# Keys and queries of two batches made ahead of the loop, and unread products on TensorE

## The chip, the core and the metric

The kernel runs on one core of a Trainium2 chip. The metric is the device time of one execution in microseconds (us). The kernel before takes 330.56 us, the median of three runs (330.47 to 331.02). The profile is one further execution of 328.42 us, whose span on the core is 326.3 us.

The engines are TensorE (PE; its weight loads are PEld), VectorE (DVE), ScalarE (ACT), GpSimd (POOL) and SyncE (SP), which only issues transfers. Each takes its instructions in the order in which the program has them and stops at a wait until a semaphore reaches a value.

## The reference, cut to what matters

```python
# x [8,112,256], ctx [8,375,256], 16 heads of 16, mask [8,1,112,375]
q = heads(layernorm(x) @ Wq + bq); k = heads(ctx @ Wk + bk); v = heads(ctx @ Wv + bv)
scores = where(mask, -1e15, q k^T / 4)
x = x + tanh(g_xattn) * (heads_back(softmax(scores) v) @ Wo + bo)
h = layernorm(x)
# router: mean over the rows -> tanh(@W1 + b1) -> @W2 + b2 -> softmax -> the best 3 of 8 zones, per batch
x = x + tanh(g_ffn) * (h + sum over those 3 zones of w * (gelu(h @ Wa[zone]) @ Wb[zone]))
```

## The kernel before

A batch is one of the eight samples. The program has two parts. A loop over `b` from -2 to 7 does attention, and at the same time turns the weights of all eight zones (`Wa`, `Wb`) into a high and a low half in fp16 that stay in SBUF. A second stage does the 24 zone products, three a batch.

The loop is pipelined by hand over batches. In iteration `b` the kernel makes the keys and queries of batch `m = b + 2`, the raw scores and row maxima (`s1`, L1016; `row_max`, L769) and the values of batch `n = b + 1`, and the transposed scores, exponentials and sums with the values of batch `b` (`st_tile`, L1028 and L1032; `exp_tile`, L545; `pv`, L1048). What belongs to the output of batch `b - 1` follows (names with `o`). So iteration -2 makes only keys and queries of batch 0, iteration -1 the scores of batch 0 with the keys and queries of batch 1 between them, and iteration 0 is the first with exponentials. Every iteration has four slots. `slot_uses` lists which small products stand in a slot, and the class `Spare` deals three PSUM banks out to them in that order; a product waits until the one that had its bank before is read.

How keys and queries are made: TensorE transposes the context (CX0, CX1, L1057) and the normalized x (XT, L1083), ScalarE and VectorE copy them out (`cx_copy`, `xt_copy`), TensorE multiplies with Wk and Wq (K0, K1, L1066; Q, L1092), ScalarE writes the fp16 high part and VectorE the low part (`k_hi`, `k_lo`, `q_hi`, `q_lo`). SyncE writes them to DRAM (`write_k`, L316; `write_q`, L310) and reads them back in another layout in two groups of six transfers (`read_k`, L339; `read_q`, L327). The first score product of a batch waits for the first group.

SyncE's queue carries nearly all transfers of the loop: these, the context (L299), x (L292) and mask (L304) of coming batches, the expert weights, two parts of 128 x 512 at a time, into a ring of six (`load_parts`, L359 and L362), and the move of the row maxima into `rq` (`move_max`, L348). The weights start in iteration -1: parts 0 to 3 are asked for in its slots 0 and 1 and worked on in slots 2 and 3. For each pair GpSimd scales (`scale_part`, L459), ScalarE rounds to the high half (`w_hi`, L655), and GpSimd subtracts to the low half (`lo_part`, L464). GpSimd scales the pair of the next slot before it makes the low halves of the present one. The normalization of x of the batch after next stands at the end of an iteration: statistics on VectorE (`ln1_stats`, L788 to L791), two operations on GpSimd (`norm1`, L469 and L470), then `normed` (L586) on ScalarE. All of this is in program order on each engine, so ScalarE starts the exponentials of iteration 0 only behind `w_hi` of parts 0 to 3 and `normed`.

The constants: ScalarE's queue loads Wq, Wk, bk, bq, bv, the gates and Wo ahead of all its work. `tanh_gates` (L611, L615) takes the gates and scales Wo at the end of iteration -2. GpSimd loads bo and the router's small weights (L502 to L506) ahead of the loop. The product of bv with Wo (BO, L1102) stands in slot 3 of iteration -1. VectorE fills five tiles with constants at the start (L897 to L902), counted by `zeroed`.

Of the kernel before, what the change touches and what calls it, by code (L numbers as in the profile page):

```python
# [11 lines left out]
ACT = mybir.ActivationFunctionType  # L12
# [48 lines left out]

def slot_uses(b, slot):

    n, m, o = b + 1, b + 2, b - 1
# [6 lines left out]
    more = {(B - 2, 3): ("H", 0), (B - 1, 0): ("L", 0), (B - 1, 2): ("W", 0), (-1, 3): ("BO", 0)}.get((b, slot))  # L71
# [16 lines left out]
class Spare:  # L88


    def __init__(self):
        names, banks = [], []
# [48 lines left out]
def flamingo_layer(nc, x, ctx, mask, g_xattn, g_ffn, Wq, bq, Wk, bk, Wv, bv, Wo, bo,  # L141
                   W1, b1, W2, b2, Wa, Wb, out):
    with ExitStack() as stack:
# [143 lines left out]
        def _(sp):  # L287
# [111 lines left out]
            load_ctx(0)  # L399
            sp.dma_start(wqkvo[:, 2, :, :], view_w(Wv)).then_inc(s["wv_loaded"], 16)  # L400
            for b in range(-2, B):
                n, m, o = b + 1, b + 2, b - 1
                read_k(n, 1)
                read_q(n, 1)
# [3 lines left out]
                load_ctx(m + 1)  # L408
                load_x(m + 1)
                load_mask(m)  # L410
                load_parts(b, 1)
# [39 lines left out]
        def _(pool):  # L451
# [46 lines left out]
            pool.wait_ge(s["zeroed"], 5)  # L498
# [3 lines left out]
            g.dma_start(bo_r[:, :], bass.AP(bo.tensor, 0, [[0, 128], [1, D]])).then_inc(s["const_loaded"], 16)  # L502
            g.dma_start(w1_s[:, :, :], W1.rearrange("(t p) n -> p t n", p=128)).then_inc(s["const_loaded"], 16)
            g.dma_start(w2_s[:, :], W2).then_inc(s["const_loaded"], 16)
            g.dma_start(b1_c[:, :], b1.rearrange("(p o) -> p o", o=1), allow_slow_non_contiguous=True).then_inc(s["const_loaded"], 16)
            g.dma_start(b2_r[:, :], bass.AP(b2.tensor, 0, [[0, B], [1, NZ]])).then_inc(s["const_loaded"], 16)  # L506
            for b in range(-2, B):
                for slot in range(4):
# [9 lines left out]
                    for k in ks:  # L518
                        lo_part(k)
            norm2(B - 2)  # L520
# [4 lines left out]
        def _(act):  # L525
            a = nc.scalar
            a.dma_start(wq_in, view_w(Wq)).then_inc(s["wq_loaded"], 16)
            a.dma_start(wqkvo[:, 1, :, :], view_w(Wk)).then_inc(s["wk_loaded"], 16)
            a.dma_start(bk_c[:, :], bk.rearrange("(t p) -> p t", p=128), allow_slow_non_contiguous=True).then_inc(s["bk_loaded"], 16)
            for t in range(DT):  # L530
                a.dma_start(bq_c[:, t:t + 1], bass.AP(bq.tensor, t * 128, [[1, HD], [HD, PAIRS], [1, 1]]), allow_slow_non_contiguous=True).then_inc(s["bq_loaded"], 16)
            a.dma_start(bv_c[:, :], bv.rearrange("(t p) -> p t", p=128), allow_slow_non_contiguous=True).then_inc(s["bv_loaded"], 16)
            a.dma_start(gates[:, 0:1], bass.AP(g_xattn.tensor, 0, [[0, 128], [1, 1]])).then_inc(s["g_loaded"], 16)
            a.dma_start(gates[:, 1:2], bass.AP(g_ffn.tensor, 0, [[0, 128], [1, 1]])).then_inc(s["g_loaded"], 16)
            a.dma_start(wqkvo[:, 3, :, :], view_w(Wo)).then_inc(s["wo_loaded"], 16)
# [38 lines left out]
            def mask_bias(b):  # L574
                if there(b):
# [3 lines left out]
                    if b == 0:  # L579
                        act.wait_ge(s["zeroed"], 5)  # L580
# [88 lines left out]
            normed(0)  # L669
            act.wait_ge(s["wq_loaded"], 16)  # L670
# [614 lines left out]
```

## Time and profile before

| what | us |
|---|---|
| median of the runs | 330.56 |
| profiled execution | 328.42 |
| its span | 326.3 |
| TensorE busy | 289.3 (89%) |
| VectorE busy | 203.2 (62%) |
| ScalarE busy | 195.5 (60%) |
| GpSimd busy | 134.3 (41%) |
| loop starts its iteration 0 (TensorE) | 42.45 |
| iteration 1 | 62.96 |
| zone products start | 198.62 |

The median lies 2.14 us above the profiled execution. Times below count from the start of the span. A row of a timeline merges equal instructions: where it starts, how long it lasts, engine and line, what it writes and reads, how many, and in brackets how long the engine stood idle before it and what ended that. PEq, SPq and ACTq are the sequencers, which issue transfers. A product of fp32 matrices counts as two instructions.

### The profile page before, as it was taken

The numbers are of one execution on the slowest core, as the hardware profiler recorded it, in microseconds if no ns is written. First come the engines' busy times: TensorE is split into PE (matmuls) and PEld (weight loads), VectorE is DVE, ScalarE is ACT, GpSimd is POOL, SyncE is SP. The second block draws the span as 40 slices with busy tenths as digits, with TensorE's granted clock in tenths as the row PEclk, the third lists the DMA queues.
The fourth block names the chain that finished last, engine by engine and source line by source line (L and its number), as shares of the span: only waits on it lengthen the run. The fifth ranks groups of instructions, "written<-read, shape, count | busy, mean of one in ns | idle before, by whom it ended". The sixth has DMA issues, their size and how long they took to land.

```text
span 326.3 us, 9360 instructions
## 1 busy us (share of the span) xinstructions
PE 289.3 (89%) x3348; PEld 242.0 (74%) x3348; DVE 203.2 (62%) x617; ACT 195.5 (60%) x406; POOL 134.3 (41%) x185
## 2 busy tenths in 40 slices
PE   1619679899989999999989867999999999999996
PEld 1406457676766766767666646999999999999996
DVE  7417838576787777877687545656564745636542
ACT  2413466877878778777787876635454753543531
POOL 3401576867778689687788871000000000000000
PEclk9978979999999999999999999999999999999999
DMA  7458776787677977868664512101110110101000
GB/s 163 123 152 234 177 226 161 214 250 182 196 206 176 274 211 191 255 182 242 180 191 145 147 44 58 33 27 33 41 33 2 44 31 17 44 2 44 2 16 14
DMA packets 39324, 40.51 MB, mean 124 GB/s; under 512 B 10249, under 2 KB 35137, under 8 KB 39281
## 3 DMA queue, kind: packets, MB, share of 16 engines
q1 hardware_dynamic: 37168, 38.94, 42.7%
q10 hardware_dynamic: 1936, 0.79, 1.0%
q8 instruction: 28, 0.46, 0.6%
q0 software_dynamic: 176, 0.20, 0.3%
q14 instruction: 16, 0.12, 0.1%
HBM read 33.09 MB, written 6.74 MB: 122 GB/s over the span
## 4 chain that ended last, share of the span: by engine, by line
PE 64%; DMA 9%; ACT 7%; DVE 5%; issue 5%; SPq 5%; POOL 2%; ACTq 0%; DVEq 0%
PE bank L1240 18%; PE bank L1221 16%; PE bank L1066 6%; PE bank L1075 4%; PE bank L1016 4%; DMA qbd<-q_scr 4%; PE bank L1028 4%; PE bank L1032 3%; PE bank L1048 3%; ACT pT L545 2%; DMA stage<-in_L_ffn_Wa 2%; PE bank L1057 2%; SPq L339 2%; PE bank L1132 2%; ACT wa L655 2%
## 5 line engine op out<-in xcount | busy, mean ns | idle before, releaser
L769 DVE CUSTOM_DVE_ANT_0 bank<-bank,maskb 112x375 f32<-112x375 f32 x128 | 67.9, 571 | 39.8 <-PE bank L1016 39.7
L1240 PE MATMUL bank<-wb,stage 128*112 x576 | 66.8, 273 | 0.0
L1240 PEld LDWEIGHTS bank<-wb,stage 128*112 128x112 f16 x576 | 62.2, 130 | 0.2
L1221 PE MATMUL bank<-ctxT,wqkvo 128*128 128x112 f16 x960 | 59.4, 213 | 2.0 <-DVE qbd L895 1.3
L1221 PEld LDWEIGHTS bank<-ctxT,wqkvo 128*128 128x128 f16 x960 | 57.5, 98 | 2.9 <-issue 2.2
L732 ACT ACTIVATE kst<-bank 128x448 f32<-128x448 f32 x48 | 25.6, 534 | 55.4 <-PE bank L1221 55.3
L545 ACT ACTIVATE pT<-bank 125x448 f32<-125x448 f32 x96 | 48.9, 539 | 9.0 <-PE bank L1032 8.3
L894 DVE COPY wqkvo<-wa 128x3072 f16 x24 | 23.2, 969 | 48.5 <-PE bank L1221 47.5
L459 POOL TENSOR_SCALAR stage<-stage 128x512 f32<-128x512 f32 x64 | 38.5, 618 | 26.5 <-DMA stage<-in_L_ffn_Wa 21.7
L1016 PE MATMUL bank<-kst,qbd 128*112 128x375 f16 x128 | 33.8, 338 | 15.2 <-DMA qbd<-q_scr 11.8
L464 POOL TENSOR_TENSOR wb<-stage,wb 128x512 f16<-128x512 f32 x32 | 37.5, 1191 | 14.0 <-ACT wb L655 14.0
L1028 PE MATMUL bank<-rq,maskb 115*128 115x448 bf16 (+1 forms) x96 | 35.5, 370 | 7.5 <-ACT pT L545 7.1
L1221 PE MATMUL bank<-ctxT,qbd 128*128 128x112 f16 x192 | 40.9, 213 | 0.0
L464 POOL TENSOR_TENSOR wa<-stage,wa 128x512 f16<-128x512 f32 x32 | 36.4, 1159 | 10.0 <-ACT wa L655 10.0
L1032 PE MATMUL bank<-qbd,kst 128*128 128x224 f16 (+1 forms) x192 | 34.4, 260 | 0.0
L958 DVE SCALAR_TENSOR_TENSOR stage<-kst,wbc,stage 128x448 f16<-128x448 f32 x48 | 30.9, 680 | 3.9 <-ACT stage L734 3.8
L734 ACT ACTIVATE stage<-kst,wbc 128x448 f16<-128x448 f32 x48 | 32.1, 669 | 1.6
L1032 PEld LDWEIGHTS bank<-qbd,kst 128*128 128x128 f16 (+1 forms) x192 | 21.6, 113 | 11.7 <-issue 1.3
L1016 PEld LDWEIGHTS bank<-kst,qbd 128*112 128x112 f16 x128 | 15.0, 132 | 19.9 <-DMA qbd<-q_scr 12.8
L1048 PE MATMUL bank<-pT,vp 125*17 125x112 f32 (+1 forms) x768 | 24.7, 261 | 0.0
L469 POOL TENSOR_TENSOR rstd<-ve,half 112x1 f32<-112x1 f32 x16 | 8.8, 551 | 37.0 <-DVE ve L791 37.0
L1028 PEld LDWEIGHTS bank<-rq,maskb 115*128 115x128 bf16 (+1 forms) x96 | 10.7, 111 | 14.9 <-ACT pT L545 12.7
(123 smaller groups left out, 423.6 us busy)
## 6 DMA issues: line engine op xcount, KB each, us to landing
stage<-in_L_ffn_Wa SPq DMA_DIRECT2D x16, 512.0 KB, 4.3
stage<-in_L_ffn_Wb SPq DMA_DIRECT2D x16, 512.0 KB, 4.4
kst<-k_scr SPq DMA_DIRECT2D x64, 93.8 KB, 3.7
k_scr<-wb SPq DMA_DIRECT2D x16, 187.5 KB
ctx_s<-in_ctx SPq DMA_DIRECT2D x8, 336.0 KB
qbd<-q_scr SPq DMA_DIRECT2D x32, 56.0 KB, 3.1
xa<-in_x SPq DMA_DIRECT2D x8, 112.0 KB, 4.4
q_scr<-wb SPq DMA_DIRECT2D x16, 56.0 KB, 3.2
```

Of the source, the lines that this page charges most:

```text
L459: g.tensor_scalar(st, st, WSCALE, 1.0, ALU.mult, ALU.mult).then_inc(s["scaled"], 1)
L464: g.tensor_tensor(part_dst(k, 1), stage[:, k % RING, :], part_dst(k, 0), ALU.subtract).then_inc(s["lo_done"], 1)
L545: a.activation(pT[0:CK, t % PRING, :], bank[0:CK, ST_BANKS[t % len(ST_BANKS)], 0:QUAD], ACT.Exp).then_inc(s["act_exp"], 1)
L734: a.activation(hT[:, u % 2, cols], h_w[:, cols], ACT.Copy, scale=wbc[:, u:u + 1]).then_inc(s["hthi_done"], 1)
L769: v.tensor_tensor_reduce(out=bank[0:SQ, e, 0:SK], in0=bank[0:SQ, e, 0:SK], in1=maskb[0:SQ, b % 2, 0:SK], scale=-1.0, scalar=FLOOR, op0=ALU ...
L958: v.scalar_tensor_tensor(out=hT[:, u % 2, (2 + hf) * QUAD:(3 + hf) * QUAD], in0=h_w[:, cols], scalar=wbc[:, u:u + 1], in1=hT[:, u % 2, col ...
L1016: T.matmul(bank[0:SQ, e, 0:SK], qbd[:, b % 2, e, p, :], kst[:, b % 2, p * SK:(p + 1) * SK], start=True, stop=True).then_inc(s["pe_s1"], 1)
L1028: T.matmul(o[0:w, :].rearrange("k (j q) -> k j q", j=4), maskb[0:KQ, b % 2, c * CK:c * CK + w], rq[0:KQ, g // 2, :, g % 2, :], start=True, ...
L1032: ins = T.matmul(o[0:w, i * 2 * SQ:(i + 1) * 2 * SQ].rearrange("k (e q) -> k e q", e=2), kst[:, b % 2, p * SK + c * CK:p * SK + c * CK + w ...
L1048: ins = T.matmul(bank[32 * j:32 * j + VC, O_BANK, g * SQ:(g + 1) * SQ], vp[0:k, b % 2, c, h, :], pT[0:k, tile(b, g, c) % PRING, j * SQ:(j ...
L1221: ins = T.matmul(o, first(ws, t, f), x2b[:, b % 2, (xs * DT + t) * SQ:(xs * DT + t + 1) * SQ], start=(t == 0 and xs == 0 and ws == 0), sto ...
L1240: ins = T.matmul(o, hT[:, u % 2, hs * FT * SQ + f * SQ:hs * FT * SQ + (f + 1) * SQ], wb[:, bass.ds(e * (4 * CHUNK) + ws * (2 * CHUNK) + f ...
```

## The change

Keys and queries of batches 0 and 1 are made in a row ahead of the loop, in the order of the list `AHEAD`, on all engines. The loop starts at -1. In iteration -1 nothing is made of keys and queries (`made(-1)` is no batch); from iteration 0 on they are made of `b + 2` as before. On SyncE the write and the reads of batch 1 stand ahead of the loop, so ahead of the first weights. Wk is loaded ahead of Wq; bk and bq move from ScalarE's queue to SyncE's, ahead of the mask of batch 0; Wv moves behind the reads of batch 0; bv, the gates and Wo move to SyncE's queue in iteration -1. GpSimd's five constant loads move to the end of iteration -1, `tanh_gates` there too, and the product BO with what VectorE does with it to iteration 0. VectorE's fills of vp and pT move behind batch 0's keys and queries. A function `busy(n)` on TensorE multiplies the identity with itself into a score bank; nothing reads the result. It runs nine times ahead of the first transposes and twelve times behind batch 1's queries.

```diff
+def made(b):
+    return b + 2 if b >= 0 else B
...
+AHEAD = (("CX0", 0), ("CX1", 0), ("XT", 0), ("K0", 0), ("K1", 0), ("Q", 0),
+         ("CX0", 1), ("CX1", 1), ("K0", 1), ("K1", 1), ("XT", 1), ("Q", 1))
...
             load_x(0)
             load_ctx(0)
+            sp.dma_start(bk_c[:, :], bk.rearrange("(t p) -> p t", p=128), allow_slow_non_contiguous=True).then_inc(s["bk_loaded"], 16)
...
+            load_mask(0)
+            load_ctx(1)
+            load_x(1)
+            write_k(0, 0)
+            write_k(0, 1)
+            write_q(0)
+            for h in range(2):
+                read_k(0, h)
+                read_q(0, h)
             sp.dma_start(wqkvo[:, 2, :, :], view_w(Wv)).then_inc(s["wv_loaded"], 16)
-            for b in range(-2, B):
-                n, m, o = b + 1, b + 2, b - 1
-                read_k(n, 1)
-                read_q(n, 1)
+            load_mask(1)
+            write_k(1, 0)
+            write_k(1, 1)
+            write_q(1)
+            for h in range(2):
+                read_k(1, h)
+                read_q(1, h)
+            for b in range(-1, B):
+                n, m, o = b + 1, made(b), b - 1
+                if n > 1:
+                    read_k(n, 1)
+                    read_q(n, 1)
                 move_max(b, 1)
                 load_parts(b, 0)
                 load_xr(o)
-                load_ctx(m + 1)
-                load_x(m + 1)
+                load_ctx(b + 3)
+                load_x(b + 3)
                 load_mask(m)
+                if b == -1:
+                    sp.dma_start(wqkvo[:, 3, :, :], view_w(Wo)).then_inc(s["wo_loaded"], 16)
...
                 load_parts(b, 1)
...
+                    if (b, slot) == (-1, 3):
+                        g.dma_start(bo_r[:, :], bass.AP(bo.tensor, 0, [[0, 128], [1, D]])).then_inc(s["const_loaded"], 16)
...
             normed(0)
+            cx_copy(0)
+            xt_copy(0)
             act.wait_ge(s["wq_loaded"], 16)
...
+            k_hi(0, 0)
+            k_hi(0, 1)
+            q_hi(0)
+            cx_copy(1)
+            mask_bias(0)
+            normed(1)
+            k_hi(1, 0)
+            k_hi(1, 1)
+            xt_copy(1)
+            q_hi(1)
+            mask_bias(1)
...
-                normed(m + 1)
-                if b == -2:
+                normed(b + 3)
+                if b == -1:
                     tanh_gates()
...
             v.memset(qbd[:].rearrange("p a e j f -> p (a e j f)"), 0.0).then_inc(s["zeroed"], 1)
+            ln1_stats(0)
+            v.memset(bank[:, O_BANK, :], 0.0).then_inc(s["zeroed"], 1)
+            v.memset(maskb[96:KQ, :, :], 1.0).then_inc(s["zeroed"], 1)
+            cx_copy(0)
...
+            def busy(n):
+                for i in range(n):
+                    T.matmul(bank[:, ST_BANKS[i % 2], 0:128], ident[:, :], ident[:, :], start=True, stop=True)
...
             pe.wait_ge(s["ident_ready"], 1)
-            pe.wait_ge(s["zeroed"], 3)
-            for b in range(-2, B):
+            busy(9)
+            for name in AHEAD:
+                put(name)
+            busy(12)
+            for b in range(-1, B):
```

What stands in a row on SyncE before, from the last read of batch 0 to the write of batch 1 (`stage` takes expert weights, `k_scr` and `q_scr` are keys and queries in DRAM, `kst` and `qbd` the tiles that they are read back to):

```order
L327 DMA qbd<-q_scr 64x1x448 x2
L359 DMA stage<-in_L_ffn_Wa 128x1024
L299 DMA ctx_s<-in_ctx 112x3x256
L299 DMA ctx_s<-in_ctx 13x3x256
L292 DMA xa<-in_x 112x256
L304 DMA mask_s<-in_mask_Bx1xSxS_bk 112x375
L359 DMA stage<-in_L_ffn_Wa 128x1024
L316 DMA k_scr<-wb 8x32x375 x2
L310 DMA q_scr<-wb 128x2x112 x2
L348 DMA rq<-ms 3x4x224
```

And now, from the same read to the first weights:

```order
L335 DMA qbd<-q_scr 64x1x448 x2
L420 DMA wqkvo<-in_L_xattn_Wv 128x2x256
L312 DMA mask_s<-in_mask_Bx1xSxS_bk 112x375
L324 DMA k_scr<-wb 8x32x375 x2
L318 DMA q_scr<-wb 128x2x112 x2
L347 DMA kst<-k_scr 32x1500 x4
L335 DMA qbd<-q_scr 64x1x448 x2
L347 DMA kst<-k_scr 32x1500 x4
L335 DMA qbd<-q_scr 64x1x448 x2
L367 DMA stage<-in_L_ffn_Wa 128x1024
```

The first weights stand directly behind batch 0's reads before, and behind batch 1's write and all twelve of its reads now. Behind them SyncE has now, to the second weights:

```order
L367 DMA stage<-in_L_ffn_Wa 128x1024
L307 DMA ctx_s<-in_ctx 112x3x256
L307 DMA ctx_s<-in_ctx 13x3x256
L300 DMA xa<-in_x 112x256
L440 DMA wqkvo<-in_L_xattn_Wo 128x2x256
L441 DMA bv_c<-in_L_xattn_bv 128x2x1
L442 DMA gates<-in_g_xattn 128x1
L443 DMA gates<-in_g_ffn 128x1
L367 DMA stage<-in_L_ffn_Wa 128x1024
L356 DMA rq<-ms 3x4x224
```

Four transfers that ScalarE's queue issued have come between, and the mask has gone. On ScalarE this stands before, from the values of batch 0 to the first exponentials (`pT`):

```order
L605 ACTIVATE vp<-bank,vsc 125x32x16
L655 ACTIVATE wa<-stage 128x512 x2
L581 ACTIVATE maskb<-mask_s 112x375
L605 ACTIVATE vp<-bank,vsc 126x16x16
L655 ACTIVATE wa<-stage 128x512 x2
L586 ACTIVATE xa<-xa,nmr,rstd 112x256
L545 ACTIVATE pT<-bank 125x448 x2
```

And now:

```order
L633 ACTIVATE vp<-bank,vsc 125x32x16
L683 ACTIVATE wa<-stage 128x512 x2
L633 ACTIVATE vp<-bank,vsc 126x16x16
L683 ACTIVATE wa<-stage 128x512 x2
L614 ACTIVATE xa<-xa,nmr,rstd 112x256
L639 ACTIVATE tgate<-gates 128x2
L643 ACTIVATE wqkvo<-wqkvo,tgate 128x512
L573 ACTIVATE pT<-bank 125x448 x2
```

The high halves of parts 0 to 3 stand ahead of the first exponentials in both; the gates and the scaling of Wo have joined them, and the mask has left.

## Rows read from the trace of the kernel before

**Rows 1.** Busy time by stretch: length, each engine (instructions), granted clock, DMA share, GB/s.
```profile
0.00:42.45 42.45, 20.88 (x86) 14.23 (x86) 23.45 (x71) 14.20 (x31) 14.62 (x32) 0.92 0.64 168
...
62.96:198.62 135.66, 126.18 (x1350) 92.22 (x1351) 97.75 (x365) 104.95 (x237) 103.78 (x133) 1.00 0.68 193
```

**Rows 2.** Timeline of TensorE.
```profile
9.98 4.25 PE L1066 MATMUL bank<-ctxT,wqkvo 128*128 128x375 f32 x8 [1.32 <-DVE ctxT L805]
...
23.63 0.87 PE L1016 MATMUL bank<-kst,qbd 128*112 128x375 f16 x2 [8.53 <-DMA qbd<-q_scr]
...
26.60 1.51 PE L1066 MATMUL bank<-wb,wqkvo 128*128 128x375 f32 x4
...
38.93 1.03 PE L1102 MATMUL bank<-wqkvo,bv_c 128*112 128x256 f32 x4
...
42.45 0.53 PE L1016 MATMUL bank<-kst,qbd 128*112 128x375 f16 x2 [2.11 <-DMA qbd<-q_scr]
...
44.64 0.58 PE L1028 MATMUL bank<-rq,maskb 115*125 115x448 bf16 x1
...
62.96 0.53 PE L1016 MATMUL bank<-kst,qbd 128*112 128x375 f16 x2 [0.78 <-DMA qbd<-q_scr]
```

**Rows 3.** Timeline of SyncE's queue.
```profile
2.19 0.41 SPq L400 DMA_DIRECT2D wqkvo<-in_L_xattn_Wv  x1
...
25.14 0.59 SPq L359 DMA_DIRECT2D stage<-in_L_ffn_Wa  x1
26.37 0.83 SPq L299 DMA_DIRECT2D ctx_s<-in_ctx  x2
...
28.10 0.43 SPq L359 DMA_DIRECT2D stage<-in_L_ffn_Wa  x1
```

**Rows 4.** The chain that ended last, in order of time: start, us, what.
```profile
15.50 4.29 DMA k_scr<-wb
...
32.47 0.61 SPq L316
```

**Rows 5.** Timeline of ScalarE.
```profile
18.73 0.19 ACT L611 ACTIVATE tgate<-gates 128x2 f32<-128x2 f32 x1
18.95 0.72 ACT L615 ACTIVATE wqkvo<-wqkvo,tgate 128x512 f32<-128x512 f32 x1
...
42.07 0.60 ACT L586 ACTIVATE xa<-xa,nmr,rstd 112x256 f32<-112x256 f32 x1 [1.43 <-POOL nmr L470]
42.57 0.52 ACT L545 ACTIVATE pT<-bank 125x448 f32<-125x448 f32 x1
```

**Rows 6.** Timeline of GpSimd.
```profile
9.81 0.81 POOL L502 DMA_DIRECT2D bo_r<-in_L_xattn_bo  x1 [0.29 <-issue]
...
33.02 1.20 POOL L459 TENSOR_SCALAR stage<-stage 128x512 f32<-128x512 f32 x2 [1.76 <-DMA stage<-in_L_ffn_Wa]
37.81 2.27 POOL L464 TENSOR_TENSOR wa<-stage,wa 128x512 f16<-128x512 f32 x2 [3.60 <-ACT wa L655]
```

**Rows 7.** Timeline of VectorE.
```profile
7.21 1.93 DVE L902 MEMSET pT<- 30x2240 f32 x1 [0.42 <-issue]
```

**Rows 8.** TensorE by stretch: length, busy time, granted clock, DMA share, GB/s.
```profile
5.00:15.00 10.00, 6.88 (x24) 1.00 0.58 144
44.64:47.00 2.36, 2.36 (x9) 0.50 0.50 122
48.00:50.00 2.00, 2.00 (x34) 1.00 1.00 290
```

**Rows 9.** The page's DMA issues: count, KB each, median us from issue to landing.
```profile
stage<-in_L_ffn_Wa SPq DMA_DIRECT2D x16, 512.0 KB, 4.3
...
q_scr<-wb SPq DMA_DIRECT2D x16, 56.0 KB, 3.2
```

**Rows 10.** Timeline of ScalarE's queue.
```profile
3.59 0.61 ACTq L532 DMA_DIRECT2D bv_c<-in_L_xattn_bv  x1
4.23 0.48 ACTq L533 DMA_DIRECT2D gates<-in_g_xattn  x1
...
5.22 0.46 ACTq L535 DMA_DIRECT2D wqkvo<-in_L_xattn_Wo  x1
```

More of the change, by code:

```diff
@@ L91, in __init__ @@
     def __init__(self):
-        names, banks = [], []
-        for b in range(-2, B):
+        names = list(AHEAD)
+        banks = [MISC_BANKS[i % len(MISC_BANKS)] for i in range(len(AHEAD))]
+        for b in range(-1, B):
             for slot in range(4):
@@ L501, in _ @@
                             base=-CK, pattern=[[0, 2], [0, NH]], channel_multiplier=1).then_inc(s["ones_ready"], 1)
[L502 to L507, printed above, removed]
+            for b in range(-1, B):
                 for slot in range(4):
@@ L526, in _ @@
             a = nc.scalar
+            a.dma_start(wqkvo[:, 1, :, :], view_w(Wk)).then_inc(s["wk_loaded"], 16)
             a.dma_start(wq_in, view_w(Wq)).then_inc(s["wq_loaded"], 16)
[L528 to L535, printed above, removed]
             def exp_tile(b, g, c):
@@ L669, in _ @@
             normed(0)
+            cx_copy(0)
+            xt_copy(0)
             act.wait_ge(s["wq_loaded"], 16)
             a.activation(wq_p[:, :, :, :], wq_in.rearrange("p k (t j i) -> p (k t) i j", t=DT, i=HD), ACT.Copy, scale=HD ** -0.5).then_inc(s["wq_scaled"], 1)
-            for b in range(-2, B):
-                n, m, o = b + 1, b + 2, b - 1
+            act.wait_ge(s["bq_loaded"], 32)
+            a.activation(bq_c[:, :], bq_c[:, :], ACT.Copy, scale=HD ** -0.5).then_inc(s["wq_scaled"], 1)
+            act.wait_ge(s["wq_scaled"], 2)
+            act.wait_ge(s["bk_loaded"], 16)
+            k_hi(0, 0)
[9 more added lines that the diff above has]
+            mask_bias(1)
+            for b in range(-1, B):
+                n, m, o = b + 1, made(b), b - 1
                 exp_tile(b, 0, 0)
@@ L897, in _ @@
             v.memset(qbd[:].rearrange("p a e j f -> p (a e j f)"), 0.0).then_inc(s["zeroed"], 1)
+            ln1_stats(0)
+            v.memset(bank[:, O_BANK, :], 0.0).then_inc(s["zeroed"], 1)
+            v.memset(maskb[96:KQ, :, :], 1.0).then_inc(s["zeroed"], 1)
+            cx_copy(0)
+            dve.wait_ge(s["wq_scaled"], 2)
+            dve.wait_ge(s["bk_loaded"], 16)
+            k_lo(0, 0)
+            k_lo(0, 1)
+            q_lo(0)
+            ln1_stats(1)
+            cx_copy(1)
             v.memset(vp[:].rearrange("p a c h i -> p (a c h i)"), 1.0).then_inc(s["zeroed"], 1)
[L899 to L901 removed]
+            k_lo(1, 0)
+            k_lo(1, 1)
             v.memset(pT[96:CK + 1, :, :], 1.0).then_inc(s["zeroed"], 1)
             dve.wait_ge(s["zeroed"], 5)
[L904 to L905 removed]
+            q_lo(1)
+            for b in range(-1, B):
+                n, m, o = b + 1, made(b), b - 1
                 row_max(n, 0)
@@ L928, in _ @@
                 x2_lo(b - 2)
-                ln1_stats(m + 1)
+                ln1_stats(b + 3)
                 row_max(n, 6)
@@ L1040, in pv @@
                     pe.wait_ge(s["act_exp"], tile(b, g, 2) + 1)
+                    if b == 0 and g == 0:
+                        pe.wait_ge(s["zeroed"], 2)
                     if g == 0:
@@ L1180, in _ @@
             pe.wait_ge(s["ident_ready"], 1)
-            pe.wait_ge(s["zeroed"], 3)
-            for b in range(-2, B):
+            busy(9)
+            for name in AHEAD:
+                put(name)
+            busy(12)
+            for b in range(-1, B):
                 for slot in range(4):
```

33 lines of the change are left out of this document (15 added, 18 removed).

## The prediction

> **What bounds the kernel now.** I read the busy time by stretch first [rows 1]. In 62.96 to 198.62, iterations 1 to 7 of the loop, TensorE is busy 126.18 of 135.66 us: it is the bound there, and the change leaves that work alone. What is idle lies in front: in 0 to 42.45 TensorE is busy 20.88 us. So I read TensorE's timeline of that stretch [rows 2]. It shows a first block of products for batch 0 (transposes, keys, queries) that ends at 15.1, a wait of 8.53 us until the keys and queries of batch 0 are back from DRAM (23.63), an iteration for the scores of batch 0 in which the keys of batch 1 are made between them, and a wait of 2.11 us until batch 1's are back (42.45). From there the loop goes at its steady pace.
>
> The reader is to see two more things, because the change moves both. First, SyncE's queue issues one transfer after the other and stops at a wait [rows 3]: each transfer costs its 0.4 to 0.6 us there even if all is ready. The write of the second half of batch 0's keys is issued at 15.50 and is on the chain for 4.29 us [rows 4]; the queue then issues twelve reads and comes to the first expert weights at 25.14. Second, the loop's first exponential starts at 42.57 [rows 5], and it stands on ScalarE behind the halves of weight parts 0 to 3 and a normalization that itself waits for GpSimd [rows 5, 6]. That chain already ends within 0.1 us of the arrival of batch 1's queries. It is no slack: what is added to it is added to the loop.
>
> **The change, part by part.** All times are of the profiled execution, 328.42 us with a span of 326.3; the median of the runs is 330.56, so 2.14 us are added at the end.
>
> 1. The first block comes earlier. VectorE no longer fills pT (1.93 us [rows 7]) ahead of its copy of the transposed context, and ScalarE's queue issues two transfers in place of nine ahead of its table load. The copy then waits only for the transposes, the statistics of x and a small fill; I put the first key product at 8.2 in place of 9.98, 1.8 us earlier. Between nothing (transposes wait for the same context and x) and 2.7 (all of the wait and the fill), this is the middle, since x's statistics and the transposes themselves don't move.
>
> 2. The key products of batch 0 take 4.25 us for eight passes, those of batch 1 1.51 us for four [rows 2], so about 1.5 us are lost to a slow start. The change runs nine unread products of 128 columns from 1.7 us on, until the context is there. I count 1.6 us saved, and bounds of 0 and 1.6. The granted clock stands at 1.00 in the rows of this stretch [rows 8], and would by itself say that there is nothing to save; the durations say half speed. The Trainium skill (TensorE: Matmul & The Clock Gate, section "What's actually happening") says that the default state is throttled and that activity releases it. By the row of the clock this term would be 0 and the sum 1.6 us more; by the rule it is 1.6. The durations of this trace side with the rule.
>
> Together the write of batch 0's second key half moves from 15.50 to 12.1, 3.4 us earlier; bounds 0 and 4.3.
>
> 3. What stands behind it in SyncE's queue. From that write to the first weights it takes 25.14 - 15.50 = 9.64 us [rows 3, 4], the landing and both groups of reads. Now the queue goes: batch 0's reads end at 12.1 + 9.64 = 21.7; the load of Wv and the mask of batch 1, 0.46 each with the gap, as Wv's 0.41 [rows 3]: 22.65. Only then may batch 1's keys be written, although they have been ready since about 18. Its first half goes out at 22.65, the second at 23.3 (0.61 each [rows 4]), and landing and twelve reads take the same 9.64: 32.9. So the first weights are asked for at 32.9, not at 25.14: 7.8 us later. Bounds of one landing: 4.29 as here, or 3.2 as the query writes of the whole run have in the middle [rows 9].
>
> 4. Between the two first weight transfers lie now context and x of batch 2 (28.10 - 26.37 = 1.73, less 0.46 for the mask, which is gone from there: 1.27 us [rows 3]), and Wo, bv and the two gates, which come over from ScalarE's queue: 0.46 + 0.61 and 0.48 twice with four gaps of 0.04, 2.19 us [rows 10], the second gate taken as the first. With the issue of the first (0.59) and its gap it is 4.1: the second weights are asked for at 37.0 in place of 28.10, 8.9 us later.
>
> 5. From there to the first exponential. The transfer lands after 33.02 - 28.10 = 4.92 us [rows 3, 6] (bound: 4.3, the middle of all of them [rows 9]): 41.9. GpSimd scales parts 2 and 3, 1.20: 43.1. Then in its order the low halves of parts 0 and 1, the scaling of 4 and 5, and the two small operations for x of batch 2, which took from 37.81 to 42.07 [rows 5, 6]: 47.35. In the kernel before this ran from 37.81 because ScalarE gave the release; now the scaling is the last of what it waits for. ScalarE normalizes (42.07 to 42.57, 0.50), then does the gates and the scaling of Wo, which stand in this iteration now: 18.95 + 0.72 - 18.73 = 0.94 [rows 5]. The exponential starts at 48.8, not at 42.57: 6.2 us later.
>
> 6. TensorE. The third score tile of the loop needs this exponential. It started at 44.64 [rows 2], 1.5 us behind the exponential's end, since TensorE had come late itself. Now TensorE waits there: 48.8 + 0.52 + 0.04 = 49.4, 4.7 us later. Everything behind it is the same work in the same order.
>
> 7. The clock. From 44.64 to 47 the granted clock is 0.50, from 48 on 1.00 [rows 8]: there the kernel before runs at 1.2 GHz, and loses some 1.2 us. In the changed kernel TensorE idles from about 45.5 to 49.4 ahead of this place. If the clock holds, the 1.2 us come back; if it falls, TensorE needs again about the 3.1 us that passed from 23.63 on, 0.4 more than before. The idle stretches in [rows 2] ended in a fallen clock both times, so I take + 0.3.
>
> 8. The bv product (1.03 [rows 2]) moves from the iteration where TensorE waits into one where it is busy, next to the wait of 0.78 us at 62.96 [rows 2] that hides most of it: + 0.1. If that wait is gone it costs 0.9.
>
> 9. The twelve unread products behind batch 1's queries last some 3 us (24 passes at the 0.13 us that passes of this width take in the row of the bv product, halved from 256 columns). They may hold the first scores, which I put at 12.1 + 8.13 = 20.2, until 22.5. Nothing pays for it, since part 3 runs on SyncE meanwhile. The five constant loads of GpSimd (0.81 the first [rows 6]) now stand behind the low halves of parts 2 and 3, in idle time of GpSimd of similar size. Both count 0.
>
> Sum: 4.7 + 0.3 + 0.1 = + 5.1 us. 328.42 + 5.1 = 333.5 in the profiled execution, 330.56 + 5.1 = **335.7** in the median. The 3.4 us won at the start are inside: they are what makes part 3 end at 32.9 and not at 36.3.
>
> **The rivals.** A, the weights are no gate (faster). If the first exponential did not stand behind weights that are asked for late, the loop would start when batch 1's queries are back: 23.3 + 8.13 = 31.4 in place of 42.45, so 11 us earlier, 319.6. For it speaks that TensorE's own work of this iteration shrinks by the keys of batch 1. Against it stands every row of parts 3 to 5. It decides if the second weights land before about 31; I give it 0.05.
>
> B, only SyncE's queue binds (slightly faster). x of batch 2 is asked for at about 34.4 and, with the 4.3 us of [rows 9], lands at 38.7; VectorE stands at its statistics ahead of the last four row maxima, so the loop can start at about 41.5 even with no weights in it. If GpSimd and ScalarE are quicker through the parts than the rows say, TensorE starts the loop where it does now and saves the slow clock only: about - 1.5, 329.1. It decides if the second weights land by 36. 0.08.
>
> C, the transfers land sooner. With 3.2 us for each of the two landings in part 3 and 4.3 in part 5, 2.2 + 0.6 us go: + 2.3, 332.9. The writes of batch 1 are not in front of a wait in this trace, so their landing is not shown; those of batch 0 took 4.29 with a light load beside them, and now batch 1's have Wv and the reads beside them, which speaks against it. 0.15. The Trainium skill (DMA: Bandwidth & Descriptors, section "Anatomy of one DMA") gives about 2.0 us plus the bytes at 436 GB/s, which is 2.4 us for a key write and 3.2 us for a weight transfer; with these the sum would be an estimate of - 0.4, about no change. The trace disagrees for the same transfers (4.29 and 4.92), so this is a chance of 0.03.
>
> D, the delay grows. GpSimd comes 6.5 us late to the low halves of parts 4 and 5, because the constant loads (some 3 to 4 us in all) stand ahead of the scaling of parts 6 and 7; SyncE waits for those halves ahead of the write of batch 2's keys. If this chain and not TensorE's 5.1 sets the start of the next iteration, it costs 1.4 more: 337.1. The row at 62.96 shows that this start already waits for the queue. Against it: the second key half of batch 2 is written 3 us behind the first, and that wait hides the excess. 0.17.
>
> **How the numbers follow.** The forecast has 0.52, A 0.05, B 0.08, C 0.15, the rule's case 0.03, D 0.17. About 0.2% is what a measurement of this kernel can tell, 0.7 us here. Faster is A, B: 0.13. Within: 0.03. Slower is the rest: 0.84. The forecast's own range comes from the early block (0 to 1.6 us of clock), the landings and the clock in the loop: 333.5 to 337.5. With C and D it is 331.5 to 338.5, which leaves A, B and a little of D outside.
>
> **What would show it.** In the changed profile: the first weights are issued near 33 and the second near 37; the keys of batch 1 are complete on ScalarE near 18 but written from 22 to 24; GpSimd's first scaling starts near 38; the first exponential is near 49 and its releaser is ScalarE's own earlier work or GpSimd; TensorE idles 3 to 5 us behind the first score tiles of the loop; and behind 70 us all intervals between iterations are as before. I am wrong if the first exponential starts before 43, if SyncE's issues are shorter than 0.4 us in this stretch, or if the steady iterations change their length.

## The result, and the profile after

The changed kernel took 340.50 us, the median of four runs (339.81 to 340.86), against 330.79 for the kernel before beside it (330.47 to 336.38). The ratio is 1.028, with an interval of 1.022 to 1.034. So the direction was right, and the time lies 4.8 us above the forecast of 335.7 and 2.0 above the upper end of its range. The profiled execution took 340.16 us with a span of 338.0, 11.7 more than before's 326.3; before's profiled execution lay 2.4 below this median, the changed kernel's 0.3 below its own, and that is the difference between 11.7 and the 9.7 of the medians. The medians hold all runs, while the ratios here and below leave out those over 1.5% above the fastest of their kernel: one of before's four here, one of four in f_order, two of six in i_order_fill, three of six in j_after_fill, one of twelve in l_before_small (744 us) and seven of twelve in k_before_24.

TensorE's timeline of the changed kernel, with start, duration and the wait ahead in brackets; it answers to [rows 2]:

```profile
1.68 4.21 PE L1219 MATMUL bank<-ident 128*128 128x128 f32 x18 [1.68 <-POOL ident L521]
...
8.98 5.03 PE L1116 MATMUL bank<-ctxT,wqkvo 128*128 128x375 f32 x8 [0.48 <-DVE ctxT L845]
...
22.45 2.86 PE L1219 MATMUL bank<-ident 128*128 128x128 f32 x24
25.14 0.48 PE L1064 MATMUL bank<-kst,qbd 128*112 128x375 f16 x2
...
44.48 1.06 PE L1064 MATMUL bank<-kst,qbd 128*112 128x375 f16 x2 [8.04 <-DVE peaks L809]
...
55.10 0.63 PE L1076 MATMUL bank<-rq,maskb 115*125 115x448 bf16 x1 [3.76 <-ACT pT L573]
...
74.35 0.53 PE L1064 MATMUL bank<-kst,qbd 128*112 128x375 f16 x2 [0.64 <-DMA qbd<-q_scr]
```

The last row is the start of iteration 1. It stood at 62.96 and stands at 74.35: 11.4 of the 11.7 us arise ahead of it. The third score tile of the loop moved from 44.64 to 55.10, by 10.5. Between the scores of batch 0 TensorE now waits 8.04 us and ahead of the third tile 3.76 us. The 8.04 us are no wait for weights: the row maxima that free TensorE's banks stand on VectorE behind the statistics of x of batch 2, and VectorE waits for that x, which SyncE asks for only at 38.64:

```profile
42.88 0.43 DVE L828 BATCH_NORM_STATS2 stat<-xa 112x6 f32<-112x256 f32 x1 [9.83 <-DMA xa<-in_x]
```

That is what rival B describes. The 3.76 us behind it are the chain of the weights. Both start in SyncE's queue; this answers to [rows 3]:

```profile
13.30 2.62 SPq L324 DMA_DIRECT2D k_scr<-wb  x2
...
25.11 0.59 SPq L420 DMA_DIRECT2D wqkvo<-in_L_xattn_Wv  x1
25.74 0.46 SPq L312 DMA_DIRECT2D mask_s<-in_mask_Bx1xSxS_bk  x1
26.25 1.28 SPq L324 DMA_DIRECT2D k_scr<-wb  x2
...
37.05 0.59 SPq L367 DMA_DIRECT2D stage<-in_L_ffn_Wa  x1
...
41.00 0.43 SPq L367 DMA_DIRECT2D stage<-in_L_ffn_Wa  x1
```

The first weights are asked for at 37.05, not at 25.14, and the second at 41.00, not at 28.10. GpSimd and ScalarE follow; first GpSimd, then ScalarE, both answering to [rows 5, 6]:

```profile
41.32 1.21 POOL L492 TENSOR_SCALAR stage<-stage 128x512 f32<-128x512 f32 x2 [21.70 <-DMA stage<-in_L_ffn_Wa]
47.76 1.20 POOL L492 TENSOR_SCALAR stage<-stage 128x512 f32<-128x512 f32 x2 [5.23 <-DMA stage<-in_L_ffn_Wa]
...
55.29 0.81 POOL L550 DMA_DIRECT2D bo_r<-in_L_xattn_bo  x1
```

```profile
53.17 0.60 ACT L614 ACTIVATE xa<-xa,nmr,rstd 112x256 f32<-112x256 f32 x1 [3.55 <-POOL nmr L503]
53.68 0.19 ACT L639 ACTIVATE tgate<-gates 128x2 f32<-128x2 f32 x1
53.90 0.72 ACT L643 ACTIVATE wqkvo<-wqkvo,tgate 128x512 f32<-128x512 f32 x1
54.52 0.96 ACT L573 ACTIVATE pT<-bank 125x448 f32<-125x448 f32 x2
```

That is the chain that the prediction named, member by member. The same is seen in the chain that ended last of the changed kernel:

```profile
15.30 4.02 DMA k_scr<-wb
...
26.91 4.85 DMA k_scr<-wb
...
41.00 6.69 DMA stage<-in_L_ffn_Wa
```

Behind iteration 1 nothing changed. By stretch, with the same columns as [rows 1] but TensorE alone; the first row answers to the 126.18 us of 135.66 there, the two last to [rows 8]:

```profile
74.35:210.01 135.66, 126.80 (x1349) 1.00 0.68 192
5.00:15.00 10.00, 8.79 (x32) 1.00 0.28 69
...
54.00:56.00 2.00, 0.90 (x4) 0.63 0.25 88
56.00:58.00 2.00, 2.00 (x7) 0.51 0.48 78
```

### The profile page after: what moved, and what is told of

Same layout as the page of the kernel before. It is cut to its first block, busy times and chain, and to the rows that moved or that the text cites. A ratio compares the mean times of both kernels' runs of the same rounds, so it can differ in the third digit from the quotient of the medians.

```text
span 338.0 us, 9444 instructions
## 1 busy us (share of the span) xinstructions
PE 303.0 (90%) x3390; PEld 250.0 (74%) x3390; DVE 203.0 (60%) x617; ACT 195.8 (58%) x406; POOL 134.4 (40%) x185
## 4 chain that ended last, share of the span: by engine, by line
PE 54%; DMA 16%; SPq 11%; POOL 6%; ACT 5%; issue 5%; DVE 3%; ACTq 0%; DVEq 0%
PE bank L1298 17%; PE bank L1279 16%; PE bank L1116 6%; DMA qbd<-q_scr 4%; SPq L347 4%; DMA stage<-in_L_ffn_Wb 3%; DMA stage<-in_L_ffn_Wa 3%; DMA k_scr<-wb 3%; SPq L335 3%; PE bank L1076 3%; PE bank L1064 2%; PE bank L1098 2%; POOL stage L492 2%; PE bank L1080 2%; POOL wb L497 2%
## 5 line engine op out<-in xcount | busy, mean ns | idle before, releaser
L1064 PE MATMUL bank<-kst,qbd 128*112 128x375 f16 x128 | 34.9, 346 | 12.4 <-DVE peaks L809 9.4
## 6 DMA issues: line engine op xcount, KB each, us to landing
k_scr<-wb SPq DMA_DIRECT2D x16, 187.5 KB
```

The source lines that it names most:

```text
L1064: T.matmul(bank[0:SQ, e, 0:SK], qbd[:, b % 2, e, p, :], kst[:, b % 2, p * SK:(p + 1) * SK], start=True, stop=True).then_inc(s["pe_s1"], 1)
```

## The experiments

A measure first. In the thirteen profiles of the table the time from the start of iteration 1 to the end is 262.0 to 267.4 us, though the work there is the same (263.3 before, 263.7 after). So one profile's span says little about an edit at the start, while the start of iteration 1 in it says much; the medians are for the verdict. Before's own profile is a quick execution (328.42, where its median is 330.56), so the distance to its "it. 1" may be too large by some of that. "Exp" is the start of the loop's first exponential, "it. 1" that of iteration 1; the ratio is to the kernel before, measured beside it.

| kernel | median us | ratio (95%) | exp | it. 1 |
|---|---|---|---|---|
| before | 330.7 to 331.2 | | 42.57 | 62.96 |
| after | 340.50 | 1.028 (1.022 to 1.034) | 54.52 | 74.35 |
| a_weights | 338.78 | 1.023 (1.018 to 1.028) | 53.81 | 73.16 |
| b_weights_x | 339.50 | 1.024 (1.018 to 1.030) | 51.48 | 71.85 |
| c_no_busy | 342.43 | 1.034 (1.030 to 1.038) | 54.47 | 75.55 |
| d_small | 335.66 | 1.015 (1.010 to 1.019) | 49.43 | 69.13 |
| e_tiny | 336.47 | 1.015 (1.009 to 1.022) | 52.97 | 72.70 |
| f_order | 327.98 | 0.987 (0.978 to 0.995) | 40.85 | 60.46 |
| g_busy9 | 341.12 | 1.032 (1.026 to 1.038) | 51.70 | 72.13 |
| h_before_busy | 327.27 | 0.989 (0.984 to 0.994) | 43.53 | 61.61 |
| i_order_fill | 328.29 | 0.986 (0.979 to 0.993) | 40.04 | 59.97 |
| j_after_fill | 342.89 | 1.027 (1.020 to 1.035) | 52.35 | 72.36 |
| k_before_24 | 330.64 | 0.990 (0.986 to 0.994) | | |
| l_before_small | 331.49 | 1.002 (0.998 to 1.005) | 46.61 | 65.04 |

**Are the late weights the cause?** a_weights asks for the first two ahead of batch 1's key write; b_weights_x also takes context and x of batch 2 along, between them.

```
             load_mask(1)
+            load_parts(-1, 0)
+            load_parts(-1, 1)
             write_k(1, 0)
...
-                load_parts(b, 0)
+                if b >= 0:
+                    load_parts(b, 0)
```

> The changed kernel with one edit: SyncE asks for weight parts 0 to 3 ahead of the write of batch 1's keys (behind the mask of batch 1) and not behind its twelve reads. Theory (the weights asked for late hold GpSimd and ScalarE, and by them the first exponential at 54.5): the first scaling of GpSimd starts near 31 and not at 41.3, the first exponential is then held by x of batch 2 and the row maxima behind it, near 49 to 50; 335.5 us, 5 less than the changed kernel. Rival (TensorE itself, its slow clock and the queries of batch 1, sets the start of the loop): 340.5, as now.

> As a_weights, and context and x of batch 2 are asked for there too. Theory (the order of SyncE's queue is the whole loss): the row maxima of batch 0 end by 37, the loop starts when the moved row maxima land, its first exponential near 43 to 44; 329 to 330 us, 11 less than the changed kernel. Rival (other costs of the change, as the bv product in the loop and the slow clock, make up half of it): 334 to 335.

Measured: 338.78 and 339.50, little better than the change itself. The early weights did what they should: in a_weights they were issued at 25.78 and GpSimd scaled them at 31.28. Yet the exponential started at 53.81. The chain of a_weights:

```profile
27.39 7.63 DMA k_scr<-wb
...
44.70 5.66 DMA stage<-in_L_ffn_Wb
...
50.44 1.20 POOL stage L496 x2
```

The key write, issued right behind 1 MB of weights, took 7.63 us to land, not 4.85 (7.70 in b_weights_x, behind the same weights with context and x). The wait on it sits in the same queue, so the twelve reads, x of batch 2, the row maxima and the third weights (44.70) came later, and the exponential stands behind the scaling of those too. So the first two weights alone aren't the gate: the next member of the queue is there at nearly the same time. In b_weights_x x of batch 2 came in time (its statistics at 31.44, with no wait), and the exponential still started at 51.48, behind the third weights (asked for at 43.85). My theory, that their move alone would give the loss back, fell.

**What are the small loads worth?** d_small puts Wo, bv and both gates back at the start of ScalarE's queue, e_tiny only bv and the gates; l_before_small does the opposite in the kernel before (with the scaling of Wo and BO one iteration later, as in the change).

```
-                if b == -1:
-                    sp.dma_start(wqkvo[:, 3, :, :], view_w(Wo))...
-                    sp.dma_start(bv_c[:, :], ...)
-                    sp.dma_start(gates[:, 0:1], ...)
-                    sp.dma_start(gates[:, 1:2], ...)
                 load_parts(b, 1)
...
+            a.dma_start(bv_c[:, :], ...)
+            a.dma_start(gates[:, 0:1], ...)
+            a.dma_start(gates[:, 1:2], ...)
+            a.dma_start(wqkvo[:, 3, :, :], view_w(Wo))...
```

> The changed kernel with the loads of Wo, bv and the two gates back in ScalarE's queue at the start, as in the kernel before. They take four issues of SyncE ahead of the second weights, 1.9 us; the second weights landed 6.7 us after they were asked for, against 4.9 in the kernel before. Theory A (transfers of four-byte elements ahead of the weights in the same queue also hold those up): the landing goes back to about 4.9, the first exponential comes 3.7 us earlier, 336.8. Theory B (they cost their issue only, the long landing is traffic): 1.9 us earlier, 338.6.

> As d_small, but Wo (256 KB) stays in SyncE's queue ahead of the second weights; only bv and the two gates, transfers of single four-byte elements, go back to ScalarE's queue. Theory (the tiny elements hold up the weights behind them in the queue): the second weights land within 5 us of being asked for, first exponential near 50 to 50.5, 336.5. Rival (Wo's bytes ahead of them do it): the landing stays above 6, first exponential near 53, 339.

> The kernel before with one part of the change alone: Wo, bv and the gates on SyncE's queue in iteration -1 ahead of the second weights, the gates' work on ScalarE at the end of iteration -1, the bv product in iteration 0. Keys and queries stay where they were. Theory (in the kernel before the second weights land 3.6 us before GpSimd needs them, so a delay of 2 to 4 us there is hidden; what shows is the 0.9 us of the gates ahead of the first exponential and the bv product): 331.5. Rival (these transfers cost by themselves what moving them back gains in the changed kernel, 4 to 5 us): 335.

Measured: 335.66, 336.47 and 331.49. In the change these four loads cost 4.8 us of the 9.7 by the medians, the three tiny ones 4.0. The profiles show less of it: from the issue of the first weights to the exponential it takes 17.34 to 17.53 us in the four kernels with them (the changed kernel, c_no_busy, g_busy9, j_after_fill), 15.16 in e_tiny and 14.00 in d_small, so 2.3 us for the three and 3.5 for the four. The rest of d_small's early exponential is its quick first block; the rest of the medians is not located. Issuing the four accounts for 2.0 (the weights' interval is 3.95 in the changed kernel, 1.99 in d_small). The transfer behind them also lands sooner without them: by the chains of waits 5.16 us in d_small and 5.85 in e_tiny, against 6.54 to 6.73 in the same four kernels. The DMA engines while it was under way, first in the changed kernel, then in e_tiny (length, TensorE's busy time, clock, DMA share, GB/s):

```profile
42.00:44.00 2.00, 0.00 (x0) 0.50 0.50 100
44.00:46.00 2.00, 1.52 (x4) 0.50 0.45 154
46.00:48.00 2.00, 1.84 (x6) 0.50 0.89 329
```

```profile
42.00:44.00 2.00, 0.00 (x0) 0.50 1.11 281
44.00:46.00 2.00, 0.17 (x1) 0.50 0.99 365
```

With bv and the gates in the queue ahead, 100 and 154 GB/s flow for 4 us and 329 only then; without them 281 at once. The three other kernels with them show the same fall from 1 to 5 us behind the second weights' issue, with 111 to 198 GB/s. The same four loads in the kernel before cost nothing that can be measured in the runs, 0.2% with an interval of -0.2 to 0.5. Its one profile has the exponential 4.0 us and iteration 1 2.1 us later than before's. 1.2 us of that is a landing of batch 0's keys of 5.48 in place of 4.29, and before's execution was a quick one; how much is left for the loads is open. In it the second weights are asked for at 31.06 and landed by 36.81, and the chain to the exponential runs through the third (asked for at 37.19, 5.99 us), not through them. So the runs speak for a cost that hangs on the loads' place on the path, and do not prove it.

**Are the unread products worth something?** c_no_busy has neither group of them, g_busy9 the nine alone.

```
-            busy(9)
...
-            busy(12)
```

> The changed kernel without both groups of unread products. My prediction counted 1.6 us for the first group. Theory now (the nine products buy nothing, since the first block ran at half speed until about 13 us with them and without them): key products of batch 0 take 4.5 to 5 us as before, scores of batch 0 start near 23.4 and not at 25.1, and the time is the same within 0.5: 340.5. Rival (without them the clock rises later still): the first block ends 1 to 2 us later, 341.5 to 342.5.

> The changed kernel with the nine unread products and without the twelve. Without both it was 342.4, with both 340.5. Theory (the nine raise the clock for the first block in some executions, the twelve only delay the scores of batch 0 by 2 us, which nothing waits for): 340.5 or a little less. Rival (the twelve keep the clock up for the scores and by that for the loop): 342 to 342.5.

Measured: 342.43 and 341.12; the intervals of c_no_busy, g_busy9 and the changed kernel overlap in pairs, so the products are worth at most some 2 us together, which is not clear of the noise, and I can't say which group. What differs is the first block. TensorE in c_no_busy and in g_busy9:

```profile
8.86 5.03 PE L1116 MATMUL bank<-ctxT,wqkvo 128*128 128x375 f32 x8 [0.47 <-DVE ctxT L845]
```

```profile
8.03 2.76 PE L1116 MATMUL bank<-ctxT,wqkvo 128*128 128x375 f32 x8 [0.66 <-DVE ctxT L845]
```

These eight passes take 2.76 us in six of the nine profiles with the changed start and the nine products (b_weights_x, d_small, f_order, g_busy9, i_order_fill, j_after_fill), and 4.45 to 5.23 in three (a_weights, the changed kernel, e_tiny). With the nine in the kernel before (h_before_busy) it was 4.96, and without them 4.19 to 5.34 (l_before_small, before, c_no_busy, k_before_24). So the products can bring the block to full speed and don't always. The slow ones are of two kinds: in the changed kernel and e_tiny the transposes ahead of the block were slow already (the two of x took 0.58 us, against 0.36 in the quick profiles), while in a_weights they were quick (0.36) and the granted clock fell after them, to 0.50 in 9 to 11. In g_busy9 the second key half was on its way at 12.07, not at 15.30, the exponential came 2.8 us sooner and iteration 1 2.2 sooner; the span was 337.8 all the same, since that execution lost it again behind iteration 1, and the median of its six runs, 341.12, is no lower than the changed kernel's.

h_before_busy puts nine products at the start and 24 ahead of the first scores into the kernel before, k_before_24 the 24 alone.

```
+                    if (b, slot) == (-1, 0):
+                        busy(24)
```

> The kernel before with unread products alone: nine ahead of the first transposes, 24 in the wait for the scores of batch 0. Theory (the clock is a small term of its own): the scores of batch 0 start at full clock, the stretch from 23.6 to 26.7 is 1 to 1.5 us shorter, the first block 0 to 1.5 us; but the start of the loop waits for SyncE's queue, so 329.5 to 330.8. Rival (the clock hardly moves the time since transfers set both starts): 330.8 as the kernel before.

> The kernel before with the 24 unread products in its wait of 8.5 us alone, not the nine at the start. With both it is 1.1% faster. Theory A (the 24 keep the clock for the scores of batch 0 and the keys of batch 1, worth 1.5 us, and the nine bring the other half by the first block): 329. Theory B (all of it comes from the wait): 327.3. Theory C (all from the start): 330.7.

Measured: h_before_busy 327.27, ratio 0.989 with all eight runs: faster. k_before_24 has a ratio of 0.990, but by its five quickest runs alone (326.44 to 329.73); the other seven took 331.55 to 333.57, and the median of the twelve, 330.64, is that of the kernel before beside it, 330.69, whose own runs reach 333.18. So the 24 alone are not shown to gain anything, and whether the nine add to them is open. TensorE in the loop's first stretch in h_before_busy, where [rows 8] have 2.36 us at a clock of 0.50 with nine instructions, and then in l_before_small:

```profile
44.64:47.00 2.36, 2.36 (x13) 1.00 0.80 164
```

```profile
44.64:47.00 2.36, 1.62 (x13) 1.00 1.10 320
```

The clock was at its upper level there in h_before_busy. From the third score tile to iteration 1 it took 17.2 us (44.41 to 61.61), 1.1 less than before's 18.3, which is what the prediction put the slow clock of this place at (1.2). But l_before_small, with no unread product, has 1.00 there too, so the upper level of this place is not shown to come from the products, which ended 23 us earlier. Where they are seen is at the first scores: the first pair took 0.53 us in h_before_busy, 0.87 before; in 26 to 28 the clock was 0.50 again. The profile has iteration 1 1.35 us earlier; the rest of the 3.4 us between the medians is not located.

**Is it the order of the queue?** f_order keeps the keys and queries of both batches in a row ahead of the loop and orders SyncE's queue by due time: first weights at 9.51, ahead of the first key write, the second between batch 0's reads and batch 1's write, x and context of batch 2 and the third weights ahead of batch 1's reads, the row maxima between the two groups of these; the small loads are back in ScalarE's queue.

```
+            sp.dma_start(wqkvo[:, 2, :, :], view_w(Wv))...
+            load_parts(-1, 0)
             write_k(0, 0)
...
+            load_mask(1)
...
+            load_parts(-1, 1)
             write_k(1, 0)
             write_k(1, 1)
             write_q(1)
-            for h in range(2):
-                read_k(1, h)
-                read_q(1, h)
+            load_x(2)
+            load_ctx(2)
+            load_parts(-1, 2)
+            read_k(1, 0)
+            read_q(1, 0)
+            move_max(0, 0)
+            read_k(1, 1)
+            read_q(1, 1)
```

> The changed kernel with SyncE's queue in another order, nothing else: Wv and weight parts 0 and 1 ahead of the write of batch 0's keys, the mask of batch 1 ahead of batch 0's reads, parts 2 and 3 ahead of batch 1's write, x and context of batch 2 and parts 4 and 5 behind that write, the first move of row maxima between the two groups of batch 1's reads, and Wo, bv and gates in ScalarE's queue as before the change. Theory (the whole loss is the order of this queue): no weight wait on GpSimd ahead of the first exponential, the loop starts when batch 1's queries are back, near 36, first exponential near 37; 324 us, faster than the kernel before. Rival (the products in a row and the bytes in the queue keep the loop from starting before 42): 330 to 332.

Measured: 327.98, ratio 0.987 (0.978 to 0.995): faster than before, 12.5 us under the changed kernel with the same row of work on TensorE. By the medians d_small, which moves the small loads alone, has 4.8 of these, and the order of the rest 7.7. SyncE's queue and TensorE in f_order:

```profile
9.51 0.47 SPq L367 DMA_DIRECT2D stage<-in_L_ffn_Wa  x1
...
24.01 0.59 SPq L367 DMA_DIRECT2D stage<-in_L_ffn_Wa  x1
...
30.61 0.39 SPq L370 DMA_DIRECT2D stage<-in_L_ffn_Wb  x1
```

```profile
37.72 0.36 PE L1086 MATMUL bank<-rq,maskb 115*128 115x448 bf16 x1 [1.19 <-DMA rq<-ms]
...
41.43 0.40 PE L1086 MATMUL bank<-rq,maskb 115*125 115x448 bf16 x1 [1.22 <-ACT pT L583]
...
60.46 0.53 PE L1074 MATMUL bank<-kst,qbd 128*112 128x375 f16 x2 [1.48 <-DMA qbd<-q_scr]
```

The third score tile starts 3.2 us earlier than before, iteration 1 only 2.5, because the wait for its queries grew from 0.78 to 1.48: the next limit is that read. The scaling of parts 4 and 5 (low halves from 35.25) now ends the chain ahead of the exponential; a late arrival of the first two weights no longer does. f_order has the unread products too, and h_before_busy, with such products and the old order, is as fast (0.989). So the runs show what the order of the queue costs the changed kernel, and not that the row of keys gains anything over the kernel before; f_order without the products was not run.

**Does filling TensorE's gaps add to it?** i_order_fill is f_order, j_after_fill the changed kernel, each with one unread product behind each pair of score passes of iteration -1, eight in all.

```
                     s1(b + 1, 2 * slot)
+                    if b == -1:
+                        busy(1)
```

> f_order with one more unread product behind each score pair of batch 0 (eight pairs, twice a slot), where TensorE has nothing else since the keys of batch 1 no longer stand there. Theory (the change took the filling out of that stretch, the clock falls in it in every profile of the changed order and the values of batch 0 take 3.5 us in place of 1.9): the granted clock stays 1.00 to the start of the loop, first exponential 1.5 us earlier, 326.5. Rival (GpSimd and the transfers set the first exponential): 328, as f_order.

> The changed kernel with the same eight unread products in its iteration -1. Theory: the clock stays up until TensorE runs out of work near 34, but the ten idle microseconds behind it, in which the weights are waited for, are still there, and the clock falls in them: 340 to 340.5, within 0.5 of the changed kernel. Rival (the slow clock in that stretch is a good part of the loss): 338 to 339.

Measured: 0.986 against f_order's 0.987, and 1.027 against 1.028: nothing that can be measured, though the six runs of j_after_fill spread from 337.66 to 347.84. In i_order_fill the clock of 26 to 34 is 1.00 (0.57 in f_order) and the exponential starts 0.8 us earlier, but the wait for iteration 1's queries is 1.80 us. In j_after_fill TensorE waits from 34 to 42 with no instruction at all, which eight products can't cover. Its profile had the first block at full speed again, and the first weights at 34.82 in place of 37.05, the exponential at 52.35 in place of 54.52.

## Why the prediction was right in direction and 4.8 us too low

The steps, in the profiled executions:

- **Part 3, the queue.** Right. From batch 0's write to the end of its reads 9.76 us (9.64 predicted); from there to the first weights 11.99 (11.2): the second write's landing was 4.85, not 4.29, and its issues a little longer. Off by 0.9 together. d_small, a_weights, b_weights_x and f_order, taken together, show that it is this queue that sets the time.
- **Part 4, the interval of the weights.** Right: 3.95 for 4.1, and d_small took it away.
- **Parts 1 and 2, the early first block. This term failed.** 3.4 us were counted and 0.2 came: the write was issued at 15.30 in place of 15.50. The key products did start 1.0 us earlier (1.8 predicted), but they took 5.03 us, more than the 4.25 before, where I had 1.6 less. I counted the nine products as bringing full speed, the upper of my own bounds (0 and 1.6). They do in six profiles of nine. In the profile, iteration 1 started 11.4 us later where 5.1 were forecast, and 3.2 of these 6.3 us lie here. The range was too narrow for this one term: with the bound of 0 that I gave for both parts the forecast would be 335.7 + 3.4 = 339.1, above the upper end. It is not the whole miss: in g_busy9 the term came in full (the write at 12.07, where I had 12.1), and iteration 1 was still 9.2 us later than before. The 4.1 us that are left there are 1.5 in the queue (first weights at 34.36, not 32.9), 1.6 in the landing (6.54, not 4.92) and 1.1 from the third score tile to iteration 1 (19.86, where I had 18.7), less 0.1 in the interval of the weights.
- **Part 5, the landing. The second term that failed.** Size wrong: 6.69 us for 4.92, 1.8 more. The tiny loads stand ahead of it in the queue; I had counted their issue (part 4) but not what they do to the transfer behind them. Without bv and gates it took 5.85, without Wo as well 5.16. From the landing to the exponential it was as predicted, 6.8 for 6.9. So the exponential came 12.0 later, not 6.2: 3.2 + 0.9 + 1.8 - 0.1.
- **Part 6.** Right: the third score tile starts 0.58 us behind the exponential's start (0.6), and what was added to the one was added to the other.
- **Parts 7 and 8.** From the third tile to iteration 1 it takes 0.9 us more than before, where 0.4 were counted. The clock fell (0.63 and 0.51 in the rows above), as [rows 2] made me expect. The BO product stands at 72.30, ahead of a wait of 0.64 at 74.35.
- **Part 9.** Right in the sum: the first scores start at 25.14, behind the twelve products, and in c_no_busy, whose write went out 0.1 us earlier, at 23.17. So the products hold them by some 1.8 us, and nobody pays, since VectorE then stands 9.83 us for x of batch 2. The constant loads of GpSimd start at 55.29 with nobody waiting in the profile.

The rivals: A and B needed second weights landed by 31 and 36; they landed at 47.7. C needed landings of 3.2 and 4.3; they were 4.85 and 6.69. The formula of the Trainium skill (DMA: Bandwidth & Descriptors, section "Anatomy of one DMA") is a fit to transfers that GpSimd issues. Carried over to these, which SyncE issues, it gives 2.4 and 3.2 us as estimates; the measured landings decide against using it here. The mechanism of B was at work: the 8.04 us are its wait for x, asked for at 38.64 and there at 42.88, where B had 34.4 and 38.7. It put the loop's first score tile at 47.41, against 39.79 before; the weights held the third one further, to 55.10. D needed a wait that grows at iteration 1; it was 0.64 for 0.78. The Trainium skill (TensorE: Matmul & The Clock Gate, section "What's actually happening") says that the default state is throttled and that activity releases it. The runs agree so far: none of the four profiles without the nine products has the quick block, and six of the ten with them have; in the other four it took 1.6 to 1.9 times as long. The granted clock's row of 5 to 15 told nothing of it in the changed kernel, where it reads 1.00 and the block took 5.03; in a_weights it reads 0.83.

The sum was made for the profiled executions and missed the span by 6.6 us (338.0 against 331.4). In the medians it is 4.8, because the 2.1 us added for before's quick execution had no counterpart: the changed kernel's profiled execution lies 0.3 below its median. That the miss looks smaller there is luck.

Open: why the nine products free the clock in one execution and not in the next, and how the spread of 5 us behind iteration 1 comes about; no run was aimed at either. In the medians the first block's share is open too, since it is known only for the profiled executions.

## What to carry to other kernels

When a change puts two blocks of work in a row, list what the transfer queue carries between them and when each entry is due: here the row itself was free, and SyncE's queue decided between 3% slower and 1% faster; unread products in the old order gave the same 1%, so the row is not shown to be a gain of its own. Moving only the one late load uncovers the next; sort the whole queue by due time, and keep tiny loads out of it ahead of a large transfer that someone waits for. A gain from warming an engine up belongs in a sum with its whole range, from nothing to all, since it may come in one execution and not in another.

## What the runs showed of the hardware

- Loads of bv and gates, issued ahead of a 512 KB load, lengthened its landing: 6.54 to 6.73 us in four profiles, 5.85 in the one without them (e_tiny), 5.16 in the one without Wo as well (d_small).
- A 187.5 KB write landed 7.63 and 7.70 us behind its issue when 1 MB of loads was issued just ahead in the same queue (a_weights, b_weights_x); the other writes of batches 0 and 1 on the chains of waits took 3.85 to 5.82.
- The same first block of products took 2.76 us in six profiles behind nine unread products, 4.45 to 5.23 in four behind the same nine, and 4.19 to 5.34 in four without them.
- The first pair of score passes took 0.53 us behind 24 unread products and a wait of 3.00 us (h_before_busy), and 0.87 us behind a wait of 8.53 us without them. In 44.64 to 47 the granted clock was 0.50 before and 1.00 in h_before_busy, but 1.00 in l_before_small too, which has none.
